# Two transformer layers on one core: value products straight from V, and a new order around the end of attention

## The reference

```
x = x + ga * attention(layernorm(x) * (1 + ca) + sa)
x = x + gb * ffn(layernorm(x) * (1 + cb) + sb)
```

## Time and profile before

| | us |
|---|---|
| median of 3 runs | 672.17 |
| lowest and highest | 668.56 and 675.68 |
| the profiled execution's own time | 665.51 |
| its span in the profile | 663.7 |
| TensorE busy | 606.6 (91%) |
| VectorE busy | 379.0 (57%) |
| ScalarE busy | 302.3 (46%) |
| GpSimd busy | 129.3 (19%) |

### The profile page before, as it was taken

How to read it: one execution, slowest core, us unless ns; L and a number is a source line. 1 busy time by engine, 2 the same in 40 slices (tenths; PEclk the granted TensorE clock), 3 DMA queues, 4 the chain that set the end, 5 groups by cost and what they waited for, 6 DMA issues and landing times.

```text
span 663.7 us, 10873 instructions
## 1 busy us (share of the span) xinstructions
PE 606.6 (91%) x3897; PEld 471.5 (71%) x3907; DVE 379.0 (57%) x757; ACT 302.3 (46%) x462; POOL 129.3 (19%) x137
## 2 busy tenths in 40 slices
PE   3898899798999999999998897889997999999995
PEld 3777645487788888888886565543445878888884
DVE  6477535966244444544457699792358543345455
ACT  3657275554233333333333473427864643333331
POOL 4501015323122222222230000000112331222220
PEclk9999899999899999999999899898999999999999
DMA  8364454100001111111100024301210001111101
GB/s 324 98 223 173 145 162 153 50 1 25 24 26 48 47 47 47 47 47 47 47 25 0 1 69 133 121 5 62 81 56 25 1 25 47 48 47 47 43 7 63
DMA packets 22194, 44.64 MB, mean 67 GB/s; under 512 B 3632, under 2 KB 7632, under 8 KB 22160
## 3 DMA queue, kind: packets, MB, share of 16 engines
q1 hardware_dynamic: 21840, 44.05, 20.8%
q10 hardware_dynamic: 320, 0.13, 0.1%
HBM read 33.16 MB, written 11.01 MB: 67 GB/s over the span
## 4 chain that ended last, share of the span: by engine, by line
PE 67%; DVE 19%; ACT 4%; issue 4%; DMA 2%; POOL 2%; SPq 0%; DVEq 0%; ACTq 0%; POOLq 0%
PE PS L557 32%; PE PS L980 16%; DVE nmx L1531 5%; PE PS L857 3%; PE PS L827 2%; PE PS L701 2%; PE PS L703 2%; DVE x L1601 1%; PE PS L601 1%; DMA w_raw<-in_wqkv 1%; PE PS L714 1%; DVE stats L1430 1%; DVE xn L1743 1%; ACT q_masked L1129 1%; PE PS L872 1%
## 5 line engine op out<-in xcount | busy, mean ns | idle before, releaser
L1273 ACT ACTIVATE qk_hi<-xn 128x512 fp32r<-128x512 f32 x82 | 51.7, 631 | 171.0 <-DVE xn L1743 139.6
L557 PE MATMUL PS<-h_hi,wqkv_hi 128*128 128x512 f32 x304 | 102.7, 395 | 1.9 <-DVE h_lo L1464 1.3
L557 PE MATMUL PS<-h_hi,wqkv_lo 128*128 128x512 f32 x272 | 92.8, 396 | 2.6 <-DVE xn L1653 2.6
L1740 DVE TENSOR_TENSOR prs<-prs,PS 128x512 f32<-128x512 f32 x60 | 41.2, 687 | 86.8 <-PE PS L557 78.3
L1747 DVE TENSOR_TENSOR qk_lo<-xn,qk_hi 128x512 fp32r<-128x512 f32 x70 | 48.4, 692 | 47.8 <-ACT qk_hi L1273 47.8
L1269 ACT ACTIVATE prs<-PS 128x512 f32<-128x512 f32 x82 | 48.7, 594 | 48.5 <-PE PS L557 48.5
L557 PEld LDWEIGHTS PS<-h_hi,wqkv_hi 128*128 128x128 f32 x304 | 57.2, 188 | 14.0 <-DVE h_lo L1464 1.7
L557 PE MATMUL PS<-h_lo,wqkv_hi 128*128 128x512 f32 x160 | 62.9, 393 | 0.0
L557 PEld LDWEIGHTS PS<-h_hi,wqkv_lo 128*128 128x128 f32 x272 | 51.1, 188 | 14.9 <-DVE xn L1653 4.3
L1531 DVE TENSOR_REDUCE nmx<-PS 128x512 f32 (+4 forms) x96 | 54.2, 637 | 4.4 <-PE PS L719 4.3
L980 PE MATMUL PS<-wqkv_hi,qk_hi 128*128 128x256 f32 x288 | 53.5, 285 | 0.9 <-POOL qk_lo L529 0.7
(11 more groups left out here) (251 smaller groups left out, 1223.4 us busy)
## 6 DMA issues: line engine op xcount, KB each, us to landing
fw_raw<-in_ffn SPq DMA_DIRECT2D x41, 384.0 KB, 3.1
qk_slot<-rows_scr SPq DMA_DIRECT2D x32, 200.0 KB
rows_scr<-qk_hi SPq DMA_DIRECT2D x16, 256.0 KB
qk_slot<-q_scr SPq DMA_DIRECT2D x32, 100.0 KB
rows_scr<-qk_lo SPq DMA_DIRECT2D x8, 256.0 KB
wmod<-in_wmod SPq DMA_DIRECT2D x1, 1536.0 KB, 14.3
x<-in_x SPq DMA_DIRECT2D x2, 512.0 KB, 4.0
wmod<-in_wmod SPq DMA_DIRECT2D x1, 1024.0 KB, 10.8
```

The lines of the kernel that those rows point to most:

```text
L557: ins = nc.tensor.matmul(dst, left(a, c), right(b, c), start=n == 0, stop=n == total - 1)
L1273: nc.scalar.activation(hidR[b][0], hid[b], ACT.Copy).then_inc(f["hi"], 1)
L1740: tt(hid[buf] if half is None else gu[buf], gact[buf], PS[:, 5, :], ALU.mult).then_inc(f["gu"], 1)
```

## The change

V gets a seventeenth column of ones. TensorE takes `V[:, kb, unit, :]`, 17 columns, as the stationary operand and writes 17 of a tile's 32 PSUM rows. `take_values`, the `Vs` tiles and their semaphore go. POOL's start loses 16 small memsets and gains one. The gates of layer 0 are copied after the second exponential, and TensorE waits for that copy only before the first value products. Dummy activations load the Exp table before `max_high` of batch 1 and the Silu table right behind the last exponential. The third weight split moves forward, and with it the two weight loads on SP. VectorE's order at the end of the pass changes, and so does TensorE's: `early_up(0)` stands ahead of the last chunk of batch 1's output projection. The diff, cut to its core:

```diff
-        V = sb("V", [P, NT, UNITS, DH])
-        Vs = [sb(f"V_slot{s}", [P, NT, VW]) for s in range(2 * SLOTS)]
+        V = sb("V", [P, NT, UNITS, DH + 1])
...
                         load_keys_major(l, u)
-                        if u in (H + 5, H + 10):
-                            s = (u - H) // 10
+                        if u in (H + 1, H + 5):
+                            s = (u - H) // 4
                             load_ffn(l, 1, s, 2 + s)
...
             def attention(l):
-                if l == 0:
-                    pool.wait_ge(v_taken, 2 * B)
-                    take_values(0)
                 for g in range(QUADS):
-                    if l == 0 and g + 1 < QUADS:
-                        take_values(g + 1)
+                    if g in (2, 3, 4):
+                        weights_low(l, g - 2, g % 2)
                     if g % 2:
                         out_low(l, g // 2)
-                    if g in (2, 3, QUADS - 2):
-                        i = min(g - 2, 2)
-                        weights_low(l, i, i % 2)
...
                     if l == 0:
-                        pe.wait_ge(a["vs"], SLOTS * (g + 1))
+                        if g == 0:
+                            pe.wait_ge(gate_taken, 2)
...
-                            v = Vs[slot][:, kb, :]
+                            v, rows = V[:, kb, SLOTS * g + s, :], DH + 1
                         else:
                             col, n = START1[kb], S - kb * P
-                            v = V1[:, kb, g // BQ, :]
-                        ins = nc.tensor.matmul(PS[s * VW:(s + 1) * VW, O_BANK[l][g % 2], kb * P:kb * P + n], v,
+                            v, rows = V1[:, kb, g // BQ, :], VW
+                        ins = nc.tensor.matmul(PS[s * VW:s * VW + rows, O_BANK[l][g % 2], kb * P:kb * P + n], v,
...
                 pe.wait_ge(at[l]["mlo"], B)
-                if l == 0:
-                    pe.wait_ge(gate_taken, 2)
...
                 project_out(l, 1, range(OC - 1), False)
+
+            def out_projection_rest(l):
                 pe.wait_ge(at[l]["ol"], CHUNKS)
                 project_out(l, 1, range(OC - 1, OC), False)
...
                 early_up(0)
+                out_projection_rest(l)
                 early_up(1)
...
+            def exp_table():
+                nc.scalar.activation(table_in[:, :], ct[:, 0, 0, 0:1], ACT.Exp)
...
             mask_rest(0, 1)
+            exp_table()
             max_high(0, 1)
...
-                    gates(0)
                     act.wait_ge(split, 3)
...
-                    if u in (2 * n - 1, 3 * n - 1, 7 * n - 2):
-                        i = u // n - 1 if u < 4 * n else 2
+                    if l == 0 and u == 1:
+                        gates(0)
+                    if u in (2 * n - 1, 3 * n - 1, 4 * n + 1):
+                        i = (u + 1) // n - 2
                         weights_high(l, i // 2, i % 2)
+                nc.scalar.activation(table_in[:, :], ct[:, 0, 0, 0:1], ACT.Silu)
...
                 norm_scales(n, slice(0, 1))
+                normalise(n)
                 outputs(l, BQ + 1)
-                normalise(n)
                 outputs(l, BQ + 2)
+                h_low(n, 0)
                 outputs(l, BQ + 3)
-                h_low(n, 0)
+                early_product(l, 0)
```

More of the change, by code:

```diff
@@ L70 @@
 EU = 2 * EARLY
-CONSTS = 34
+CONSTS = 19
 RSQRT_MAGIC = float(0x5F3759DF)
@@ L201, in build @@
         cselR = sb("cselR", [SELK, 2, P], F32R)
-        cB = [[V[:, 2 * b + h, :, :].rearrange("p u d -> p (u d)") for h in range(2)] for b in range(B)]
+        cB = [[V[:, 2 * b + h, :, :].rearrange("p u d -> p (u d)")[:, 0:S] for h in range(2)] for b in range(B)]
         csel_raw = pr[1][0:SELK, 3 * KEYS0 + 3 * P:3 * KEYS0 + 5 * P]
@@ L261, in build @@
             at.append({n: sem(f"at{l}_{n}") for n in (
-                "qk0", "qk1", "qk2", "qk3", "qm", "s", "mxd", "mt", "mhi", "mlo", "mw0", "mw1", "st", "p", "vs", "o", "oe",
+                "qk0", "qk1", "qk2", "qk3", "qm", "s", "mxd", "mt", "mhi", "mlo", "mw0", "mw1", "st", "p", "o", "oe",
                 "rd", "on", "od", "oz", "oh", "ol")})
@@ L451, in _ @@
             for tile in [cparts[:, :, :, :], V1[:, :, :, :], zeroR[:, :].bitcast(F32), k1[:, :, :].bitcast(F32), zeroB[:, :]] \
-                    + [t[:, :].bitcast(F32) for t in qk] + [t[:, :, :] for t in Vs]:
+                    + [t[:, :].bitcast(F32) for t in qk]:
                 nc.gpsimd.memset(tile, 0.0).then_inc(consts, 1)
@@ L462, in _ @@
             nc.gpsimd.tensor_copy(cselR[:, :, :].rearrange("p h q -> p (h q)"), csel_raw).then_inc(consts, 1)
-            pool.wait_ge(consts, CONSTS - 12)
-            for tile in [V1[:, :, :, DH:DH + 1]] + [t[:, :, DH:DH + 1] for t in Vs]:
+            pool.wait_ge(consts, CONSTS - 5)
+            for tile in (V1[:, :, :, DH:DH + 1], V[:, :, :, DH:DH + 1]):
                 nc.gpsimd.memset(tile, 1.0).then_inc(consts, 1)
@@ L482, in ge @@
                     pool.wait_ge(s, value)
-            def take_values(g):
-                if g >= 2:
-                    pool.wait_ge(at[0]["o"], g - 1)
-                for s in range(SLOTS):
-                    nc.gpsimd.tensor_tensor(Vs[SLOTS * (g % 2) + s][:, :, 0:DH], V[:, :, SLOTS * g + s, :],
-                                            zeroR[:, 0:NT * DH].bitcast(F32).rearrange("p (t d) -> p t d", d=DH), ALU.add)\
-                        .then_inc(at[0]["vs"], 1)
             def out_low(l, c):
@@ L1640, in attention_outputs @@
                 last()
-                early_product(l, 0)
                 norm_scales(n, slice(1, B))
```

## The result

| | before | changed |
|---|---|---|
| median, measured side by side (13 executions each) | 671.30 us | 675.15 us |
| lowest and highest | 665.36 and 680.03 | 671.41 and 682.17 |
| the profiled execution's own time | 665.51 | 671.41 |
| its span | 663.7 | 669.6 |
| its mean granted TensorE clock | 0.984 | 0.968 |

The ratio is 1.0066, with a 95% interval of 1.0037 to 1.0094: within 1%, on the slower side. The changed kernel was measured once more beside the experiments: 673.16 against 674.46, ratio 1.0012 (0.9973 to 1.0052). The forecast was 673.8 us and "within 1%".

The account below looks back on a forecast made before the run. TensorE, busy 91%, was taken as the bound. Terms -0.8 (head), +4.6 (rows), 0, -0.1, 0, -1.4 and -0.7 (ends) gave +1.6, a 665.3 us span and 673.8 us median; own range 671 to 676, 8-in-10 range 666 to 679.

Parts of the forecast that it names:

- The place of the loss: Layer 0's SyncE queue: weight load waits for its split, delaying pair 9's rows; TensorE waits 4.2 us, whole term +4.6.
- one landing (5.24): Layer 0: pair 11's rows landed 5.24 us after the weight load's issue before; the same delay was assumed for pair 9.
- The 0.8 at pair 11: Layer 0: TensorE waits for pair 11's rows behind the second weights, between 0 and 1.7 us, taken as 0.8.
- In layer 1 nobody waited for the rows: Layer 1: pair 9's rows behind the weight load would cost 0, upper end 0.6 us.
- The clock: Rival, 24%: the wait at pair 9 also lowers TensorE's granted clock, costing 1.7 us, for 675.5 us in all.
- a sign of being wrong: The prediction would be wrong if, among other signs, TensorE's granted clock fell where it did not before.
- The rival's test: The slower clock was to follow if TensorE's wait in layer 0's pass exceeded about 3 us.
- The head: Start of layer 0's pass: table loaded earlier and gates moved bring the third exponential sooner, -0.8 us.
- The table: ScalarE's table load costs 1.28 us by the trace, not the skill's 2.7; taking it off layer 1's path gives -0.1.
- Seventeen columns: Value products of layer 0 keep 1.40 us per 32 records with 17 columns: 0 us.
- The end: After the last exponentials, batch 1's transposes start sooner: -1.4 us in layer 0, -0.7 in layer 1.
- The sum: All terms together +1.6 us: span 665.3, own time 667.1, plus 6.7 to the median, 673.8 us.

Follow-up runs that it names:

- e4: Kernel before with only the new layer 0 weight loads, third weight split and GpSimd split order: 683.55 us against 675.40, ratio 1.0074.
- e3: Changed kernel with 18 unused filler matmuls on TensorE inside layer 0's wait for pair 9's rows: 673.38 us, 0.9981 of the kernel before.
- e8: Kernel before with only the 17-column values of layer 0, without GpSimd's copies: 671.97 us against 675.94, ratio 0.9992.
- e10: Kernel before with only layer 0's gates moved behind the second exponential, no table loaded ahead: 673.78 us against 674.46, ratio 1.0042.
- e2: Changed kernel with GpSimd's low weight splits one quad sooner, ahead of out_low: 666.35 us, 0.9871 of the kernel before.
- e9: Kernel before with 8 unused filler matmuls in TensorE's 1.84 us wait for layer 0's first exponentials: 667.82 us against 674.46, ratio 0.9925.
- e7: Kernel before with only layer 0's gates behind the second exponential and the Exp and Silu tables loaded ahead: 666.18 us against 675.94, ratio 0.9950.
- e1: Changed kernel with layer 0's weight loads, the third weight split and GpSimd's split order put back: 664.05 us, 0.9868 of the kernel before.
- e5: e1 with layer 1's old VectorE order, outputs before normalise, also put back: 660.23 us, 0.9839 of the kernel before.
- e6: Kernel before with only the new VectorE and TensorE order at the end of the values, both layers: 673.91 us against 675.94, ratio 1.0022.
- e12: e5 with 3 unused filler matmuls ahead of pair 4's keys in layer 0: 659.77 us, 0.9824 of the kernel before.

## Why the prediction was right, and where it was not

**The place of the loss.** Right. SyncE stands at the split, and TensorE waits 4.47 us at pair 9 against 4.2. With the old 0.40 gone the term is 4.1, inside its ends of 3.8 and 5.5. The second profile's (6.56 - 0.40 = 6.2) lies outside them: one landing (5.24) was a thin basis, and 5.5, 5.6, 7.3 (e4) and 7.6 have been seen since. The 0.8 at pair 11 did not come in the changed kernel (a wait of 0.84 did in e3). In layer 1 nobody waited for the rows: 0 forecast, right.

**The clock.** It was a rival at 24%, priced at 1.7 us from one short fall. Both profiles have it, and the prediction named it as a sign of being wrong. It costs 3.5 us (e3) to 4.1 in the first profile and 1.7 in the second. The step that failed is taking the length of a fall from another stretch: 3.4 us there, 13.6 and 10.2 here. The rival's test, a hole of over about 3 us, is too high as well: falls began within 2 us behind waits of 1.84 us (e4, e8), 1.50 (e10) and 0.75 (e2). And neither stretch of the earlier trace rows bears on waits for a DMA, as the prediction has it: TensorE waited for GpSimd at 129 to 132, and 1.53 us for ScalarE ahead of 174.

**The head.** First keys to third exponential: 3.42 us (81.76 - 78.34) against 4.48, so 1.06 won and 0.8 forecast. Its worth was something else, a stall that no longer makes the clock fall (e9; e7 agrees). I had looked at the stall only as path, and the profile of before, with its full clock behind it, could not show it. This is the term of the sum that was mis-sized most: 0.8 against 3 us (the ratio of e7) or 5 (that of e9).

**The table.** The load is off the path, and costs what the trace had, 1.28: in e10 the exponential begins 1.30 us behind the load's start. In layer 1, 0.1 forecast, nothing seen: the first exponential still waits for TensorE.

**Seventeen columns.** 1.39 us for 32, and e8 at 0.9992. Right.

**The end.** From the last exponential's end (128.52 + 0.81 = 129.33) to batch 1's transposes: 19.1 us against 21.2 before, -2.1 with -1.4 forecast. The wait there is 1.02 with 1.2 forecast. Layer 1: last exponential at 509.82, transposes at 528.98, 19.2 against 20.7, -1.5 with -0.7 forecast. But the same reorder makes `values(6)` wait 1.96 us in layer 1, and before it was 0.66:

```profile
496.63 0.62 PE L857 MATMUL PS<-prs,V 128*32 128x512 f32 x2 [0.66 <-DVE o_parts L1547]
```

There both quads write one bank and the transpose that empties it now stands behind `normalise`. The layer 1 pass is 1.4 us longer, and the gain is gone. I named what `outputs(7)` loses and did not ask who waits for `outputs(5)`.

**The sum.** 665.3 us of span were forecast and 669.6 measured, 4.3 too few. With what the profile has, the terms are -1.1 (head), +4.1 (rows), +3.5 to 4.1 (clock), -2.1, -1.5 and +1.4 (ends, `values(6)`): +4.3 to +4.9 where the span grew by 5.9. The rest lies between the passes: that stretch is only 0.2 us shorter though the end alone gives 2.1, and this profile has 20.5 us at 1.2 GHz there, that of before 13.7. No experiment ties that to the change. On the other side I added 6.7 us as the distance of a typical execution from the profiled one, and for the changed kernel it was 3.7 (675.15 - 671.41). The two errors nearly cancel: the time is right to 0.2% by luck, by a sum that lacked the clock on both sides. As a difference of the two kernels +1.6 us was forecast, and +4.4 (the ratio 1.0066) and +0.8 (1.0012) were measured. The kernel before, stalled in the head, loses some 5 us to that stall's clock by the ratio of e9; the change takes that stall away and puts another, 20 us later, in its place.

**Open.** What ends a long fall. And why e1, e2 and e5, with the same head, differ in having one: a stall makes a fall more likely, and does not decide it. The profiles hold a hint on what else does. In some a short fall lies just ahead of the pass and in others not; TensorE's last products there, in the kernel before and in e4:

```profile
74.39 5.39 PE L601 MATMUL PS<-wmod,o_parts 128*128 128x256 f32 x16
```

```profile
75.06 3.70 PE L600 MATMUL PS<-wmod,o_parts 128*128 128x256 f32 x16
```

Of the eight profiles with the longer time (before, both of the changed kernel, e3, e5, e6, e7, e12) one, e6, has a fall that begins in the first 6 us of the pass; of the six with the shorter (e1, e2, e4, e8, e9, e10), four have (e2, e4, e8, e10). No run was made to test it, and one profile per kernel is little.

## What to carry to other kernels

Where one queue issues both what is urgent and what waits for another engine, an item moved forward is paid by everything behind it: find when its semaphore is signalled, not only when its turn comes. Look at an idle stretch of TensorE twice, once as time and once as clock: filling 1.84 us of idling, with the path as long as before, was worth 0.75% of the kernel (e9). Filling with products that nobody reads tells the two apart for the price of one line. And look at the granted clock of many executions before you trust the one that was profiled.

## What the runs showed of the hardware

- **Falls of the clock are far longer in the values pass of layer 0 than elsewhere.** There TensorE stayed at 1.2 GHz for 6.8 us in e8, 10 to 17 us in the changed kernel, e2 and e6, and 37.5 and 44.3 us in e4 and e10, also where its records show it busy all the time (17.00 of 17.00 us in e2's stretch). Between the passes most falls last 3 to 4 us, none over 8. The Trainium skill ("TensorE: Matmul & The Clock Gate", What's actually happening) says that activity releases the throttle; in this pass activity alone did not, for that long.
- **Executions with a mean clock of 0.955 or less** were 24 of 81 of the kernel before, 5 of 12 of e4, 3 of 12 of e6, 4 of 12 of e8, 4 of 13 of e10: 40 of 130 with a head stall of 1.50 us or more. Of the 86 executions of the kernels with 0.75 us or less there was none. The line at 0.955 was drawn afterwards; drawn at 0.959 the counts are 46 of 130 and 5 of 86.
- **VectorE beside GpSimd.** In layer 1 the four parts of `normalise` take 1.38 us in the changed kernel, with GpSimd idle. In e5 GpSimd writes low parts meanwhile:

```profile
498.03 3.85 DVE L1452 TENSOR_SCALAR xn<-x,mv,rs 128x256 f32<-128x256 f32 x4
```

```profile
498.19 1.38 POOL L487 TENSOR_TENSOR qk_lo<-o_parts,qk_hi 128x512 fp32r<-128x512 f32 x1 [14.73 <-DVE qk_hi L1558]
499.54 1.86 POOL L508 TENSOR_TENSOR q_masked<-fw_raw,q_masked 128x768 fp32r<-128x768 f32 x1
```

The excess is 2.5 of 3.85 us, and one of the four parts takes 1.91 us in place of 0.41, about as long as GpSimd's second instruction. The Trainium skill ("SBUF — State Buffer", Who interferes with whom) says that a VectorE `tensor_scalar` in a two-port mode and GpSimd block each other for whole instructions; the rows agree. It may be why layer 1's end won more than forecast; no run took it apart.
